# Four seams of a graph network kernel: weights turned on TensorE, rings cleared in earlier passes, targets' scores gathered first, eight row buffers in the heads pass

## The reference

```
def _L1_gnn_ref(h, W_fc, attn_l, attn_r, W_res, src, dst):   # H = 12 heads of D = 64
    hh = h.reshape(n, H, D)
    ft = jnp.einsum('nhd,ed->nhe', hh, W_fc)
    a1 = jnp.einsum('nhd,hd->nh', ft, attn_l)
    a2 = jnp.einsum('nhd,hd->nh', ft, attn_r)
    e = jax.nn.leaky_relu(a1[src] + a2[dst], negative_slope=NEG_SLOPE)
    m = jax.ops.segment_max(e, dst, num_segments=n)
    ee = jnp.exp(e - m[dst])
    denom = jax.ops.segment_sum(ee, dst, num_segments=n)
    alpha = ee / denom[dst]
    agg = jax.ops.segment_sum(alpha[:, :, None] * ft[src], dst, num_segments=n)
    res = jnp.einsum('nhd,ed->nhe', hh, W_res)
    return jax.nn.relu((res + agg).reshape(n, H * D))
```

## Time and profile before

| what | us |
|---|---|
| median of three runs (3816.74 to 3828.18) | 3817.73 |
| the profiled execution, its own time | 3819.96 |
| its span, first to last instruction | 3818.0 |
| TensorE busy in the span | 3544.9 |
| DVE, ACT, POOL busy | 2428.9, 1380.7, 1112.7 |

### The profile page before, as it was taken

The page is one execution under the profiler, slowest core; times in us unless marked ns, Lnnn a source line. Parts: engine busy times, 40 slices in busy tenths (PEclk is TensorE's granted clock), DMA queues, the critical chain, the costliest instruction groups (busy, mean ns, idle before and its releaser), DMA issues. The chain is left out here.

```text
span 3818.0 us, 64399 instructions
## 1 busy us (share of the span) xinstructions
PE 3544.9 (93%) x21125; PEld 3356.4 (88%) x21125; DVE 2428.9 (64%) x4799; ACT 1380.7 (36%) x1888; POOL 1112.7 (29%) x1533
## 2 busy tenths in 40 slices
PE   7999999999999999169996999996999998899999
PEld 6999999999999655049995999996999997899999
DVE  4877886148524599338884777775444443677777
ACT  2222232222222355026663444443333333344443
POOL 6540200414521100448883222222222221222221
PEclk9999999999999999589997999998999999999999
DMA  4777987658754698336663333333333333455554
GB/s 114 240 229 217 235 248 244 197 188 254 228 196 150 194 308 284 90 101 215 219 221 122 124 124 128 128 128 135 116 128 124 128 129 141 139 182 181 183 187 144
DMA packets 363376, 672.37 MB, mean 176 GB/s; under 512 B 100181, under 2 KB 193010, under 8 KB 363242
## 3 DMA queue, kind: packets, MB, share of 16 engines
q1 hardware_dynamic: 248154, 441.01, 37.5%
q10 hardware_dynamic: 70160, 155.79, 10.6%
q0 software_dynamic: 44928, 73.84, 6.9%
HBM read 429.79 MB, written 346.94 MB: 203 GB/s over the span
## 5 line engine op out<-in xcount | busy, mean ns | idle before, releaser
L716 DVE TENSOR_TENSOR fr_lo<-fr_turned_ps,fr_hi 128x768 fp32r<-128x768 f32 x158 | 150.4, 952 | 239.2 <-ACT fr_hi L1142 239.2
L2408 DVE SCALAR_TENSOR_TENSOR c3a_y<-c3a_prod,dinv,next_const 128x768 f32<-128x768 f32 x79 | 80.4, 1017 | 288.8 <-PE c3a_prod L2566 288.8
L1286 PE MATMUL fr_prod<-fr_w_hi,fr_hi 128*128 128x396 f32 x948 | 256.8, 352 | 0.0
L1286 PE MATMUL fr_prod<-fr_wu_hi,fr_hi 128*128 128x396 f32 x948 | 254.7, 349 | 0.0
L2566 PE MATMUL cv_prod<-next_w_hi,cv_hi 128*128 128x384 f32 x948 | 249.0, 344 | 0.0
L1286 PE MATMUL fr_prod<-fr_w_lo,fr_hi 128*128 128x396 f32 x948 | 248.9, 344 | 0.0
L2566 PE MATMUL c3a_prod<-next_w_hi,c3a_hi 128*128 128x384 f32 x948 | 248.9, 344 | 0.0
L2566 PE MATMUL c3b_prod<-next_w_hi,c3b_hi 128*128 128x384 f32 x948 | 248.8, 344 | 0.0
L1286 PE MATMUL fr_prod<-fr_w_hi,fr_lo 128*128 128x396 f32 x948 | 248.8, 343 | 0.0
L1286 PE MATMUL fr_prod<-fr_wu_lo,fr_hi 128*128 128x396 f32 x948 | 248.2, 343 | 0.0
L1286 PE MATMUL fr_prod<-fr_wu_hi,fr_lo 128*128 128x396 f32 x948 | 247.7, 342 | 0.0
...
## 6 DMA issues: line engine op xcount, KB each, us to landing
...
```

The source lines that it names most:

```text
L716: v.tensor_tensor(lo[:, s2, :, :], turned_ps[:, 0:KC, :], hi[:, s2, :, :].bitcast(F32), ALU.subtract).then_inc(split_done, 1)
L1286: made = nc.tensor.matmul(prods[s2][:, bank, 0:c1 - c0], l[:, s2, s, :], w[:, s, c0:c1], start=(s == 0 and i == 0), stop=(s == KC - 1 and ...
L2408: v.scalar_tensor_tensor(y3, p3, g["dinv"][:, bass.ds(t, 1)], c3, ALU.mult, ALU.add).then_inc(prod_read, 1)
```

## The change

It has five parts.

1. **Weights.** `W_fc` and `W_res` are loaded as they lie, on the diagonal of a new tile `w_h`, by POOL in the update pass. At the start of the heads pass TensorE turns the two 128 x 128 tiles into PSUM and ACT copies them to `w_st`.
2. **Clearing.** The ring `more` becomes one tile for the heads pass and the three conv layers, cleared by POOL in the update pass. `rows` of the conv layers is cleared by DVE at the start of the heads pass. The clearings at the start of the heads pass and of cv, and the waits for them, are gone.
3. **Scores.** In the third layer the 20 gathers of `at_dst` are issued before the 20 of `rows_x`. DVE waits for the targets alone and makes `zo`, `own6` and `z_t`, which TensorE turns; then DVE waits for the rows and makes `z`, which is turned on its own.
4. **Rows of the heads pass.** `row` has eight buffers (`WIDE`), so SP may be eight tiles ahead.
5. **Unrolling.** The heads pass writes out 8 tiles, then loops 8 rounds of eight, then writes out seven. The rings `more`, `ix` and `x_o` stay at four, indexed by `slot % UNROLL`.

```diff
-def over_tiles(eng, step, drain=0):
+def over_tiles(eng, step, drain=0, unroll=UNROLL):
...
+        g["more"], g["w_h"] = sb("more", [P, UNROLL, AGG_W]), sb("w_h", [P, 2, P])
...
+        g["rows"] = sb("rows", [P, S2, D])
         heads_pass(nc, g, a, x1, agg, x2[0:N, :])
...
-        g["more"], g["rows"] = sb("more", [P, UNROLL, D]), sb("rows", [P, S2, D])
-        conv_layer(nc, g, "cv", x2, x3[0:N, :], a["L2_gnn_W"], a["L2_gnn_b"], res=x2, first=True)
+        conv_layer(nc, g, "cv", x2, x3[0:N, :], a["L2_gnn_W"], a["L2_gnn_b"], res=x2)
@@ update_pass, POOL @@
             nc.gpsimd.memset(g["rows_x"][:, :, :], 0.0).then_inc(rows_cleared, 1)
+            nc.gpsimd.memset(g["w_h"][:, :, :], 0.0).then_inc(w_zero, 1)
+            pool.wait_ge(w_zero, 1)
+            for k, w in enumerate((a["L1_gnn_W_fc"], a["L1_gnn_W_res"])):
+                for q in range(2):
+                    pool.dma_start(g["w_h"][64 * q:64 * q + 64, k, 64 * q:64 * q + 64], w).then_inc(w_in, 16)
+            nc.gpsimd.memset(g["more"][:, :, :], 0.0).then_inc(rows_cleared, 1)
+            pool.wait_ge(w_in, 64)
@@ third_layer, POOL, DVE, TensorE @@
             for c in range(SC):
+                fetch(sc3, g["dst_i"][:, c:c + 1], at_dst[:, c, :], dst_in)
+            for c in range(SC):
                 fetch(x1, g["src_i"][:, c:c + 1], rows[:, c, :], rows_in)
-                fetch(sc3, g["dst_i"][:, c:c + 1], at_dst[:, c, :], dst_in)
...
             dve.wait_ge(up, 1)
-            link(v.tensor_copy(zr[:, :], pa[0:R, 0:J * P]))
             link(v.tensor_copy(zor[:, :], pa[0:R, 256:256 + J * P]))
             link(v.tensor_copy(own_r[:, :], pb[0:R, 0:P]))
+            dve.wait_ge(rows_in, 16 * SC)
+            link(v.tensor_tensor(z[:, :, :], heads(rows, D), heads(at_dst, H), ALU.add))
+            v.scalar_tensor_tensor(z[:, :, :], z[:, :, :], SLOPE, z[:, :, :], ALU.mult, ALU.max).then_inc(scored, 1)
+            dve.wait_ge(up, 2)
+            link(v.tensor_copy(zr[:, :], pa[0:R, 0:J * P]))
@@ heads_pass: SP, POOL, DVE, ACT, TensorE @@
-            sp.wait_ge(w_zero, 1)
-            with nc.allow_non_contiguous_dma(reason="small transposed loads"):
-                for k, w in enumerate((a["L1_gnn_W_fc"], a["L1_gnn_W_res"])):
-                    for q in range(2):
-                        sp.dma_start(w_st[64 * q:64 * q + 64, k, 64 * q:64 * q + 64], w.rearrange("e d -> d e")).then_inc(w_in, 16)
...
-                if at_least(t, UNROLL):
-                    sp.wait_ge(prod_read, t - UNROLL + 1)
+                if at_least(t, WIDE):
+                    sp.wait_ge(prod_read, t - WIDE + 1)
...
-            nc.gpsimd.memset(w_st[:, :, :], 0.0).then_inc(w_zero, 1)
-            nc.gpsimd.memset(more[:, :, :], 0.0).then_inc(cleared, 1)
-            pool.wait_ge(cleared, 1)
...
-            dve.wait_ge(cleared, 1)
+            v.memset(g["rows"][:, :, :], 0.0).then_inc(cleared, 1)
             own(0, 0, 0)
...
+            act.wait_ge(w_up, 1)
+            nc.scalar.activation(w_st[:, :, :].rearrange("p k c -> p (k c)"), prods[0][:, 0, 0:2 * P], ACT.Copy).then_inc(w_turned, 1)
...
-            pe.wait_ge(w_in, 64)
+            for k in range(2):
+                made = nc.tensor.transpose(prods[0][:, 0, k * P:(k + 1) * P], g["w_h"][:, k, :], g["ident"][:, :])
+            made.then_inc(w_up, 1)
+            pe.wait_ge(w_turned, 1)
@@ conv_layer, POOL and DVE @@
-            if first:
-                pool.wait_ge(cleared, 2)
-            if first:
-                v.memset(rows[:, :, :], 0.0).then_inc(cleared, 1)
-                v.memset(more[:, :, :], 0.0).then_inc(cleared, 1)
```

91 lines of the change are left out of this document (46 added, 45 removed).

## The result

The changed kernel took 3809.48 us (median of 7 runs, 3806.77 to 3813.95), the kernel before, run beside it, 3821.48 (7 runs, 3816.74 to 3828.18). The ratio is 0.9969 with a 95% interval of 0.9958 to 0.9981, so it is faster by 12 us, or 0.3%. Forecast were 3798.5 us and 19.2 us of gain, with a range of 3793 to 3807: the sign is right, the size is not. The base of the forecast, 3817.73, was a median of 3 runs; of the 11 us between forecast and result, 3.7 are this base and 7 are the sum. The 7 are what the rest of this document is about.

The account below looks back on a forecast made before the run. TensorE, busy for 93% of the span, was taken as the bound, leaving only the seams to gain: 3.3 + 8.1 + 7.8 = 19.2 us off the median of 3817.73 gives 3798.5 us, range 3793 to 3807.

Parts of the forecast that it names:

- Seam 1: Third layer's scores: targets' gathers first shorten the chain from last gather to scan; gain 3.3 us (-0.6 to 3.7).
- Seam 2: Start of the heads pass: weights turned on TensorE, clearings moved; first x 7.4 us sooner (5.4 to 9.7), sum 8.1.
- The ramp: Heads pass's first tiles: eight row buffers remove one TensorE stall waiting for x at 1720.58; 0.7 us.
- rival 4: Heads pass rows: eight buffers may bring nothing, even at the ramp; 0.7 us, inside the range, no chance given.
- Seam 3: Start of the cv layer: without clearings, SP's start to first turn falls from 42.32 to 34.55 us; gain 7.8 (6.5 to 8.2).
- The twin c3a: Start of cv: c3a, with the same weight loads, constant and row loads, taken as model; 34.55 us to first turn.
- In the update pass ...: nothing: Update pass: POOL's added clearings (0.3 and 2.7 us) and four loads, 240 us ahead of its next work, cost nothing.
- no lock: Start of the heads pass: the sum assumes DVE's 3.90 us clearing doesn't lock POOL out; a lock would lose 3.9 us.
- The change makes the layer the same program as c3a: Start of cv: only the gathers remain of the old start, so cv should take c3a's 34.55 us; gain 7.8 us.
- Rival 2: Scores and cv start: seams don't add up, late row gathers, costs that c3a hasn't; 3805.2 us, chance 6%.
- Rival 1: Start of heads pass: DVE's clearing locks POOL out (3.9 lost) or gather lands at 6.5 us (2.0 lost); 3802.4 to 3804.4, 14%.
- Rival 3: Heads pass, TensorE's loop: longer body fetched anew at 7 jumps back, 7 to 23 us; 5% for 3806 to 3817, 3% above.

Follow-up runs that it names:

- u_scores: Changed kernel with the third layer's gathers and scores back in the old order; ratio 0.9971 (0.9961 to 0.9981) against the kernel before.
- u_weights: Changed kernel with the heads pass's weights loaded as before by SP; one execution, 183.06 us from last of update to first of heads.
- m_pool: Changed kernel with the ring cleared on DVE and 64 more instructions of satisfied waits on POOL, both in the update pass; one execution, no total time given.

## Why the prediction was wrong in size and right in sign

Point by point, by the forecast's own terms:

- **Seam 1, 3.3 us: the mechanism right, a landing mis-sized.** From the block's start to the scan the gain is 61.96 - 59.83 = 2.1 us. The chain is 3.71 shorter, as reckoned (3.69). The last gather's landing takes 3.40 us instead of 2.25, where 0.4 was added for it: 0.75 short. And its issue comes 0.4 later after the block's start. To the start of the heads block it is 3.0 (153.57 to 150.58), 2.6 in the repeats, and u_scores says 3.1; behind the scan single executions differ by up to 1.7 us, so what is more than 2.1 is not shown to be the change's.
- **Seam 2, 7.4 us to the first x, seen 6.8 (7.0 in the repeats).** The gather did become the last arrival. Its landing is 1691.38 - 1686.25 = 5.1 us where I took 4.5 between 3.29 and 6.5; that is the whole difference. Beside the row loads this landing is 4.8 to 5.7 in the other kernels. The weights bound the old start (u_weights); what the moved clearing has of the 6.8 is not known. The ramp was forecast at 0.7. The stretch is 0.9 shorter, but the stall that was to go is missing in three of the five kernels with four buffers too. So the 0.7 are real in the execution from which they were read, and rival 4 is true of the others.
- **Seam 3, 7.8 us, seen 6.6.** The twin c3a was the right model for the queue: the gather after 0.76 us, the first product 8.44 us after SP (c3a: 8.31). Then the eight first products take 5.49 us, 4.82 in c3a, as the clock rises later. That is 0.7 of the 1.1 us that were missing. The windows of PE (us, busy, PEclk, DMA share, GB/s) show it at 0.50 for all of 2031 to 2036 in the changed kernel; m_pool, with the same cv layer, had it rise within its first products and needs 49.45 us to the first of cv instead of 51.0. The changed kernel first, then m_pool:

```profile
2031.00:2036.00 5.00, 5.00 (x8) 0.50 1.03 395
```

```profile
2030.60:2034.70 4.10, 4.02 (x8) 0.64 1.02 411
```

- **"In the update pass ...: nothing". This is the first step that failed.** It counted POOL's idle time and asked who waits for POOL, not what POOL's memset keeps from others: 0.7 us and more of DVE, the bound of that pass. The trace had a hint: the earlier trace rows shows the two engines excluding each other, 0.88 us for POOL's tiny operation under DVE's addition of 1.02. I then weighed only whether DVE's clearing would lock POOL out; the sum went by no lock, which no row of the kernel before shows. The run shows it: 0.19 us for each of two operations of POOL under 3.90. I did not weigh the other direction, POOL's clearing and DVE's copies. There POOL's memset had started first in the changed kernel and in u_weights, and DVE's TENSOR_SCALAR and COPY take 0.83 and 0.69 us, or 2.33 and 2.19, for 0.23 and 0.15. Why the one clearing holds up the other engine and the other doesn't, no trace here shows.
- **The conv passes and the head of c3b, not in the sum at all. This is the larger failure of the mechanism.** "The change makes the layer the same program as c3a" is true of its instructions, but not of where tiles lie and where the code falls. Addresses: 1.5 us. Code: 1.3 us at c3b's first copy, of which 1.0 is the scatter's landing; with the gain of 0.4 ahead of it and the clock behind it, 1.7 by the table (0.7 + 1.5 less 0.5 of addresses). That where the code falls is the cause is shown by the paddings; how a block on q14 comes to hold up the landing is not. Rival 2 came nearest, with "costs that c3a's hasn't" and 3805.2 us, 12.5 of gain, which is about what came; but its reasons (late row gathers, an unexplained start) are not these.
- **Rival 1 is false** in its first half (no lock: 0.19 us each under 3.90), and true by a third in its second: the gather lands after 5.1 us, not 6.5.
- **Rival 3 is false.** In 1712 to 2000 us of the changed kernel TensorE is busy for all 288.00 us; the windows (busy of TensorE, weight loads, DVE, ACT, POOL):

```profile
1712.00:2000.00 288.00, 288.00 (x2601) 288.00 (x2600) 251.95 (x653) 190.84 (x217) 205.90 (x289) 1.00 0.66 215
```

  288.00 / 2601 x 36 = 3.99 us a tile: a body of 576 instructions jumps back without a gap. I looked for a cost where the change had put the new code, on TensorE; it came 1500 us later, on engines whose programs had only been shifted or lengthened. That a jump back has to wait for a fetch was an assumption of the rival's. No trace here shows such a wait: TensorE's loop jumps without a gap, while q8 brings 5 blocks in these 288 us (2 before), and the 0.25 us at POOL's jump over a skipped loop in c3a have no block on q14 in the 16 us before them, only one behind. That the same jump on DVE takes 0.39 or 0.25 us by the place of the code is shown, but not why.

The sum with what was measured: 3.0 + 6.8 + 0.9 + 6.9 = 17.6, less 1.6 for the update pass (0.7 to 1.0 of it the lock, the rest its first two intervals, which vary by themselves), 1.5 for the addresses and 1.7 for c3b: 12.8 us, against 13.0 in the traces and 12.0 in the medians. Of the 19.2 forecast, then, 1.6 were missing at the seams, where three landings or clocks were mis-sized, and 4.7 were lost where the forecast had nothing. That the sign came out right is the seams; that it stayed so is no merit of the sum, which had no term for the losses.
